# One wait of TensorE, the order of four copies, and a last chunk in two halves, in the feed-forward stage of an eight-core transformer layer

## What is computed

```
x = x + layernorm(attention(layernorm(x), Wq, bq, Wk, bk, Wv, bv))
# attention: 16 heads of 64; blocks of 64 tokens see the first, the last and
# three neighbouring blocks; the first and the last block see all of them
h = layernorm(x)
gate = h @ wg.T ; up = h @ wu.T          # 1024 -> 3072, integer weights / 127
x = x + layernorm((silu(gate) * up) @ wd.T)   # 3072 -> 1024
```

## Time and profile before

| | us |
|---|---|
| median of 2 runs | 2363.56 (2363.18 to 2363.95) |
| profiled execution | 2363.05 |
| its span, slowest core (5) | 2361.5 |
| spans of the other cores | 2350.5 to 2361.2 |

### The profile page before, as it was taken

How to read it: one execution, slowest core, us unless ns; L and a number is a source line. 1 busy time by engine, 2 the same in 40 slices (tenths; PEclk the granted TensorE clock), 3 DMA queues, 4 the chain that set the end, 5 groups by cost and what they waited for, 6 DMA issues and landing times.

```text
span 2361.5 us, 31390 instructions; the slowest of 8 cores (2350.5 to 2361.5 us)
## 1 busy us (share of the span) xinstructions
PE 1652.5 (70%) x11234; PEld 803.4 (34%) x11234; DVE 851.1 (36%) x2276; ACT 587.0 (25%) x794; POOL 339.0 (14%) x510
## 2 busy tenths in 40 slices
PE   0059999977777772000001999999999999999994
PEld 0024444435544441000000444444444444444442
DVE  3414334334434445646663202322223131223223
ACT  2420111154466650112222101212111111112121
POOL 2011221201211112000000202111111212121110
PEclk9999999977776666555555999999999999999997
DMA  9942432312111107996665936675766758765752
GB/s 224 267 112 56 90 72 67 105 53 84 67 60 56 56 21 152 207 200 133 154 152 134 102 32 59 94 89 65 115 62 120 76 107 76 120 62 96 85 68 102
DMA packets 359497, 239.33 MB, mean 101 GB/s; under 512 B 313008, under 2 KB 314672, under 8 KB 357296
## 3 DMA queue, kind: packets, MB, share of 16 engines
q0 software_dynamic: 225456, 111.33, 33.7%
q1 hardware_dynamic: 120064, 92.43, 16.6%
q10 hardware_dynamic: 13824, 33.56, 4.2%
HBM read 205.53 MB, written 75.63 MB: 119 GB/s over the span
## 4 chain that ended last, share of the span: by engine, by line
PE 43%; DVE 6%; DMA 6%; SPq 2%; ACT 2%; issue 1%; ACTq 1%; DVEq 0%; POOL 0%; POOLq 0%
PE gp L925 15%; PE upp L930 14%; PE yp L941 7%; DMA xn_d<-p_xn 4%; PE upp L941 4%; PE gp L941 4%; SPq L652 2%; DMA p_ctx<-ctxT_d 2%; DVE p_x L734 1%; ACT p_xn L804 1%; DVE bst3b L740 1%; DVE bst3b L742 1%; DVE y_sb L1005 1%; DVE p_attn L696 1%; DVE p_attn L694 1%
## 5 line engine op out<-in xcount | busy, mean ns | idle before, releaser
L925 PE MATMUL gp<-x2T,wg_sb 128*128 128x512 bf16 x1536 | 373.0, 387 | 407.8 <-DMA wu_sl<-wuT 387.7
L930 PE MATMUL upp<-x2T,wu_sl 128*128 128x512 bf16 x1536 | 364.2, 380 | 0.0
L925 PEld LDWEIGHTS gp<-x2T,wg_sb 128*128 128x128 bf16 x1536 | 151.8, 99 | 596.9 <-issue 422.3
L993 DVE TENSOR_TENSOR hswb<-upp,sgbuf 128x512 bf16<-128x512 f32 x192 | 132.7, 691 | 554.9 <-PE upp L930 533.8
L864 POOL DMA_DIRECT2D wu_sl<-wuT x192 | 168.1, 879 | 956.9 <-PE upp L930 574.6
L555 ACT ACTIVATE arenaB<-pp 128x768 bf16<-128x768 f32 (+2 forms) x312 | 232.2, 1068 | 145.8 <-PE pp L512 145.8
L970 ACT ACTIVATE sgbuf<-gp 128x512 bf16<-128x512 f32 x192 | 114.6, 597 | 568.0 <-PE gp L925 567.9
L930 PEld LDWEIGHTS upp<-x2T,wu_sl 128*128 128x128 bf16 x1536 | 150.9, 98 | 183.6 <-issue 4.4
L392 PE MATMUL qp<-xn1T,wq_sb 128*128 128x512 bf16 x512 | 122.6, 383 | 127.6 <-DMA xn1T<-xn_d 125.7
L512 PE MATMUL pp<-qt_buf,kt_buf 64*64 64x64 bf16 (+2 forms) x3232 | 156.3, 310 | 76.4 <-ACT arenaB L555 64.1
L941 PE MATMUL yp<-wd_sb,hswb 128*128 128x512 bf16 x768 | 197.1, 379 | 8.4 <-DVE hswb L993 8.4
(11 more groups left out here) (84 smaller groups left out, 1214.1 us busy)
## 6 DMA issues: line engine op xcount, KB each, us to landing
wu_sl<-wuT POOLq DMA_DIRECT2D x192, 256.0 KB, 4.7
xbuf<-x_in SPq DMA_DIRECT2D x32, 512.0 KB, 11.7
p_x<-x_in SPq DMA_DIRECT2D x32, 512.0 KB, 10.4
x_d<-p_x ACTq DMA_DIRECT2D x32, 512.0 KB, 6.9
x1f<-x_d SPq DMA_DIRECT2D x32, 512.0 KB, 5.2
out<-ostage POOLq DMA_DIRECT2D x32, 512.0 KB, 4.8
ctxT_d<-cstage POOLq DMA_DIRECT2D x128, 65.0 KB, 2.0
xn_d<-xn1buf ACTq DMA_DIRECT2D x32, 256.0 KB, 7.7
```

What stands on the lines that cost most here:

```text
L925: mm = te.matmul(gsl, wg_sb[:, dc * FF + hc * 128:dc * FF + (hc + 1) * 128], xsl(dc), start=(dc == 0), stop=(dc == 7))
L930: mm = te.matmul(usl, wu_sl[:, (hc % 4) * 1024 + dc * 128: (hc % 4) * 1024 + (dc + 1) * 128], xsl(dc), start=(dc == 0), stop=(dc == 7))
L993: v.tensor_tensor(hswb[:, hc * 512:(hc + 1) * 512], upp[:, (ghc % 2) * 512:(ghc % 2 + 1) * 512], sgbuf[:, (ghc % 2) * 512:(ghc % 2 + 1) * ...
```

## The change

Three edits, all in `_p4`.

1. TensorE waits at the head of chunk c for all four copies of the chunk before (`s_yraw` at 4c), not for two; the wait is there for c = 0 too, for a value of zero.
2. VectorE copies in the order 0, 1, 2, 3, and the statistics of a tile wait for its own copy.
3. The down projection of the last chunk is done for tiles 0 and 1 first, over all 24 blocks, and then for tiles 2 and 3; `s_dpe` rises after each half, and the copies of tiles 0 and 1 wait for the first half alone. All other chunks keep one group of four tiles.

```diff
                     te.wait_ge((sm.s_x2t0, sm.s_x2t1)[c % 2], 16 * 8 * (c // 2 + 1))
-                    if c >= 1:
-                        te.wait_ge(sm.s_yraw, 4 * c - 2)
+                    te.wait_ge(sm.s_yraw, 4 * c)
@@
-                    for hc in range(24):
-                        for tt in range(4):
-                            tgt, off = y_tgts[tt]
-                            for half in (0, 1):
-                                mm = te.matmul(
-                                    tgt[:, off + half * 512:off + (half + 1) * 512],
-                                    hswb[:, hc * 512 + tt * 128:hc * 512 + (tt + 1) * 128],
-                                    wd_sb[:, hc * DM + half * 512:hc * DM + (half + 1) * 512],
-                                    start=(hc == 0), stop=(hc == 23))
-                    mm.then_inc(sm.s_dpe, 1)
+                    tt_groups = ((0, 1, 2, 3),) if c < NC4 - 1 else ((0, 1), (2, 3))
+                    for tts in tt_groups:
+                        for hc in range(24):
+                            for tt in tts:
+                                tgt, off = y_tgts[tt]
+                                for half in (0, 1):
+                                    mm = te.matmul(
+                                        tgt[:, off + half * 512:off + (half + 1) * 512],
+                                        hswb[:, hc * 512 + tt * 128:hc * 512 + (tt + 1) * 128],
+                                        wd_sb[:, hc * DM + half * 512:hc * DM + (half + 1) * 512],
+                                        start=(hc == 0), stop=(hc == 23))
+                        mm.then_inc(sm.s_dpe, 1)
@@
                 def y_copies(c):
-                    v.wait_ge(sm.s_dpe, c + 1)
-                    for tt in (2, 3, 0, 1):
+                    for tt in range(4):
                         gt = 4 * c + tt
+                        if c < NC4 - 1:
+                            v.wait_ge(sm.s_dpe, c + 1)
+                        else:
+                            v.wait_ge(sm.s_dpe, c + 1 + tt // 2)
                         if gt >= 4:
                             v.wait_ge(sm.s_s5b, gt - 3)
@@
-                        v.wait_ge(sm.s_yraw, 4 * c + (3, 4, 1, 2)[tt])
+                        v.wait_ge(sm.s_yraw, gt + 1)
                         v.bn_stats(bst4[:, p2 * 12:p2 * 12 + 6], y_sb[:, sl:sl + 512])
```

## The result

| | before | after |
|---|---|---|
| median of the runs | 2363.95 us | 2385.86 us |
| profiled execution | 2363.05 us | 2385.86 us |
| its span, slowest core | 2361.5 us (core 5) | 2384.3 us (core 2) |

The ratio of after to before is 1.0098, 95% interval 1.0065 to 1.013: slower by about 23 us, in an interval of 15 to 31 us. Executions in which one die was disturbed (2500 us and more) are in the medians but not in the ratio; two of the changed kernel that the ratio counts, at 2399 and 2401 us, were slightly disturbed too (clock near 0.839 on two cores, about 0.85 on the others), and without them the means differ by about 19 us. The forecast was 2380.5 us in a range of 2375 to 2387.5.

What follows compares the result with a forecast made beforehand. PE was taken to set the feed-forward stage's pace, idling at chunk borders for copies into y_sb. Border idle +15.8, tail -2.3 and clock +3.6 summed to +17.1 us, giving 2380.5 us, range 2375 to 2387.5.

Steps and rivals of the forecast that it cites:

- The idle at the borders: At seven chunk borders PE waits for the fourth copy, 2.26 us later than the second: +15.8 us.
- The order of the copies costs nothing: VectorE copying 0, 1, 2, 3 decides nothing at a border once all four are waited for; statistics wait for nothing.
- The last chunk in two halves: yp copies run under the last down projection's second half, leaving two copies after it: -2.3 us; PE pays 0.
- The clock, +3.6: Longer idle lowers PE's clock before each of seven restarts: 14.5 us lost against 10.9, +3.6, bounds -1.1 to +10.0.
- The sum: Whole kernel: 15.8 - 2.3 + 3.6 = +17.1 us, giving 2380.5 us, 0.7% longer; chance 0.86.
- The clock better off than before: Longer rest lets PE restart at full clock at borders: +3.5 us, 2367 us; chance 0.04.
- The copies not deciding: x2T or a weight slice releases PE at the chunk head, leaving only the tail's -2.3 us: 2361.3 us; chance 0.02.
- The clock low for longer: Each border start costs 3.0 us, clock 0.57 over 7 us: +25.5 in all, 2389 us; chance 0.06.
- the rule of the Trainium skill: Idle gaps over a limit between today's and the new one halve PE's clock: +14.5 for +3.6, ending at 2391.5 us.
- Slower by over 2%: Half clock after each border restart runs on into the chunk, from +47.3 us in all; chance 0.02.

Runs made afterwards that it cites:

- the filler: Changed kernel plus 15 unread matmuls on PE at each border after the first copy, before waiting for all four: stretch 1062.3 us, ratio to before 1.0013.
- the two other kernels with as much idle as before: Kernel before with only the last chunk split: stretch 1057.5 us, ratio 1.0002; kernel before with every chunk split and a four-copy wait: 1059.9 us, ratio 0.9983.
- the two with 5.1 us per border: The changed kernel, stretch 1078.6 us, ratio 1.0098; and the kernel before with only the wait raised to four copies, stretch 1081.0 us, ratio 1.011.
- 8 us of idle taken away at the borders: Kernel before, waiting for one copy at the chunk head and the second between first gate and up groups: stretch 1041.0 us, ratio 0.9928.
- the kernel that has no idle there: Kernel before with every chunk's down projection in two halves, tiles 2 and 3 first, still waiting for two copies: median 2328.28 us, ratio 0.9855.
- with three copies: Kernel before with only the wait at the chunk head raised from two to three copies: stretch 1072.8 us, ratio 1.0069.

## Why the prediction was right, and where it was off

- *The idle at the borders, 7 x 2.26 = +15.8.* Right to the tenth: 36.0 - 20.2 = 15.8 us, and PE follows the fourth copy by 0.35 us. The wait alone, measured by itself, adds the same idle.
- *The order of the copies costs nothing.* Right: with the old order and the wait for four, the idle is the same 36.0 us.
- *The last chunk in two halves, -2.3.* Right: 2.28 us from the first copy to the statistics in place of 4.54; the yp copies followed the tail at once and ended (2335.57 + 2.35 = 2337.92) 16.2 us before the last matmul's end, where 16 were worked out. They start near 2336 and not near 2328: this core began the stage 1.5 us later and had lost more clock by then, and the 17 us that were added there hold the -2.3 us too, which comes only behind these copies. PE pays nothing for the split: the last down projection takes 41.6 us with and without it.
- *The clock, +3.6.* The mechanism was right: the clock has now fallen before every restart, and the filler takes the loss away. But the term was mis-sized: measured +6.0. Two readings went into it. The loss of today was taken from four cores, said to be those that the trace shows in full; it shows all eight, and their mean is 10.4 us rather than 10.9. And the price of a start from the low level was taken from eight starts after the long idle ahead of the stage, 2.07 us on average and 1.40 to 2.73 single; the changed kernel's borders are no such mixed sample but cost 16.5 / 7 = 2.35 us, nearly alike. The term lies inside its bounds of -1.1 to +10.0. How far off the forecast was is itself uncertain: the two other kernels with as much idle as before lost 11.6 and 13.2 us, and the two with 5.1 us per border 16.5 and 16.2, so from one profiled execution to another the term is between +3.0 and +6.1.
- *The sum.* +17.1 was forecast, +19.4 is measured in the stage. The rest of the 22.8 us between the two profiled spans, 3.4 us, comes from comparing two different cores: the slowest core began the stage at 1293.7 us rather than 1292.2 (1.5 us), and the stretches of these two cores, 1079.4 and 1058.3, are a little above and a little below the means (1.7 us more). The interval of the ratio, 15 to 31 us, holds both the forecast and the stage's 19.4 us.
- *The rivals.* The clock better off than before: excluded by 56 low borders of 56. The copies not deciding: excluded by the wait alone. The clock low for longer, to clock 0.57 over 7 us at each border: not seen; core 2, the lowest, has 0.62 to 0.66. The case for it was put a little too low: a border at 0.57 occurs before on five of the eight cores, not on three. By the rule of the Trainium skill ("TensorE: Matmul & The Clock Gate", section "HAM oscillation — how this bites in real kernels") today's idle was allowed and the new one not, +14.5 us; the measured +6.0 disagrees, since 49 of the 56 borders of before, at 2.9 us of idle, already ran on at the low clock. The rule's other half, that the new idle loses the clock, agrees with all 56 borders of after. Slower by over 2%: the low clock never held into a chunk. The long low stretch that was brought up for it is misread a little: between 560 and 905 us the digits of the earlier trace rows are 7 and 6, and the fives come behind that, where PE hardly works.

## What to carry to other kernels

A wait on the engine that sets the pace costs what the other engine still has to do when the pace-setting one has run out of work, whatever number of copies the wait names: order the work so that what the next stage needs is finished first and its copies run under the rest. Count the clock on top of the idle: here 8 us of idle taken away at the borders gave back 18 us, and the 8 of the next step cost 14. Where an idle can't be removed, filling it with useless matmuls gave back 16.3 of the 16.5 us of low clock; the kernel that has no idle there is still 37 us shorter in the stage (1025.2 against 1062.3).

## What the runs showed of the hardware

The loss of clock came in a step between 1.8 and 2.9 us of idle, ahead of and behind dense matmuls. At 1.8 us the clock stayed at 1.00 at 56 borders of 56; at 2.9 us it fell at 49 of 56, and in the two other kernels with this idle at 53 and at 56 of 56; at 4.0 and 5.1 us at all 56. Each fall is to the lower of the two levels, 1.2 GHz (8 matmuls of 512 columns in 3.36 us rather than 1.72), and costs 1.3 to 3.0 us behind the start.

What I had not expected is how alike the borders of the changed kernel are. On core 0 the last starts lie 133.13 and 133.12 us apart, and the clock over the 8 us behind all seven is 0.70; on the other cores it drifts to 0.70 or 0.71 within a few borders from as far as 0.66 and 0.79. Where the clock behind a border is lower, the next one comes later (core 2: 133.44 us at 0.66, 133.12 at 0.70), and the two seem to settle against each other; with three copies a pattern of three borders repeats on core 7 instead (0.81, 0.69, 0.63). That this is what ties them together was not tested.

```profile
1958.80 1.44 PE L924 MATMUL gp<-x2T,wg_sb 128*128 128x512 bf16 x3 [5.15 <-DVE y_sb L1009]
```
```profile
2091.93 1.44 PE L924 MATMUL gp<-x2T,wg_sb 128*128 128x512 bf16 x3 [5.15 <-DVE y_sb L1009]
```
```profile
2225.05 1.44 PE L924 MATMUL gp<-x2T,wg_sb 128*128 128x512 bf16 x3 [5.15 <-DVE y_sb L1009]
```
